# Attention's prologue: four projection banks, masks behind the first two x, and the third half's projections between units of the first pass

## What is computed

```python
x_proj = x @ Wqkv + bqkv
q = x_proj[:, :, :C].reshape(B, n_head, T, hd)
k = x_proj[:, :, C:2 * C].reshape(B, n_head, T, hd)
v = x_proj[:, :, 2 * C:].reshape(B, n_head, T, hd)
att = jnp.einsum('bhtd,bhsd->bhts', q, k) * (1.0 / jnp.sqrt(jnp.float32(hd)))
att = jnp.where(causal, att, jnp.float32(-jnp.inf))
att = jax.nn.softmax(att, axis=-1)
y = att @ v
```

## Time and profile before

| | us |
|---|---|
| median of three runs | 4287.35 (4271.38 to 4290.11) |
| the profiled execution | 4282.62 |
| its span in the trace | 4280.6 |

### The profile page before, as it was taken

How to read it: one execution, slowest core, us unless ns; L and a number is a source line. 1 busy time by engine, 2 the same in 40 slices (tenths; PEclk the granted TensorE clock), 3 DMA queues, 4 the chain that set the end, 5 groups by cost and what they waited for, 6 DMA issues and landing times. The chain is left out here.

```text
span 4280.6 us, 82568 instructions
## 1 busy us (share of the span) xinstructions
PE 3904.8 (91%) x28814; PEld 2547.7 (60%) x28814; DVE 2990.3 (70%) x7504; ACT 2260.4 (53%) x4454; POOL 1340.7 (31%) x1724
## 2 busy tenths in 40 slices
PE   5997899998399999999999999999999996999997
PEld 4886666665255555555555555555555553666664
DVE  6996456565287787777777777777777772466565
ACT  0110455555145666666665666666666663555554
POOL 2332132232524343233432434334342310132322
PEclk9998899999689999999999999999999998999999
DMA  1333111111666686766767767677776631021111
GB/s 56 98 101 96 35 60 47 53 55 35 133 87 109 100 119 103 116 96 98 114 98 102 117 102 107 101 115 105 105 120 104 100 48 56 30 65 55 59 35 45
DMA packets 701476, 361.45 MB, mean 84 GB/s; under 512 B 305072, under 2 KB 668080, under 8 KB 701104
## 3 DMA queue, kind: packets, MB, share of 16 engines
q1 hardware_dynamic: 701104, 356.65, 46.8%
HBM read 204.49 MB, written 150.99 MB: 83 GB/s over the span
## 5 line engine op out<-in xcount | busy, mean ns | idle before, releaser
L1600 DVE TENSOR_REDUCE att_maxima<-att_s 128x1 f32<-128x512 f32 (+3 forms) x3072 | 1523.6, 550 | 421.3 <-PE att_s L1776 224.4
L1698 ACT ACTIVATE att_probs<-att_s 128x512 f32<-128x512 f32 (+1 forms) x2560 | 1330.7, 557 | 896.5 <-PE att_s L1776 507.7
L1830 PE MATMUL att_s<-att_qs,att_ks 49*128 49x512 f32 (+3 forms) x3072 | 1002.2, 402 | 71.9 <-DVE att_maxima L1600 40.9
L1806 PE MATMUL att_s<-att_ks,att_qs 48*128 48x512 f32 (+3 forms) x3072 | 997.7, 409 | 2.1 <-DVE att_maxima L1600 1.6
L1830 PEld LDWEIGHTS att_s<-att_qs,att_ks 49*128 49x128 f32 x3072 | 474.4, 186 | 631.4 <-ACT att_probs L1698 409.2
L1858 PE MATMUL att_o_ps<-att_probs,att_vs 128*32 128x512 f32 (+3 forms) x6144 | 637.4, 500 | 6.0 <-issue 5.5
L1776 PE MATMUL att_s<-att_mask,att_places 64*128 64x64 bf16 (+1 forms) x5632 | 591.8, 209 | 1.8 <-issue 1.8
L1806 PEld LDWEIGHTS att_s<-att_ks,att_qs 48*128 48x128 f32 x3072 | 506.0, 188 | 17.0 <-DVE att_maxima L1600 8.5
L1070 PE MATMUL ffn_h2p<-ffn_h,ffn_w 128*128 128x512 f32 x768 | 382.1, 622 | 2.3 <-ACT ffn_h L947 0.5
L1776 PEld LDWEIGHTS att_s<-att_mask,att_places 64*128 64x128 bf16 x5632 | 284.0, 96 | 113.3 <-issue 43.1
L1517 POOL TENSOR_TENSOR att_x_res<-att_x_res,att_bp_row 128x512 f32<-128x512 f32 x64 | 81.5, 1284 | 772.9 <-DMA att_x_res<-x 770.0
(11 more groups left out here) (227 smaller groups left out, 5782.7 us busy)
## 6 DMA issues: line engine op xcount, KB each, us to landing
att_staged<-qk_scratch SPq DMA_DIRECT2D x768, 128.0 KB, 7.2
qk_scratch<-att_parts SPq DMA_DIRECT2D x128, 512.0 KB, 2.9
ffn_x<-x SPq DMA_DIRECT2D x64, 512.0 KB, 4.9
ssm_x<-in_L_attn_a_x_dram SPq DMA_DIRECT2D x32, 512.0 KB, 3.9
x<-ssm_y SPq DMA_DIRECT2D x32, 512.0 KB, 2.9
x<-ffn_y SPq DMA_DIRECT2D x32, 512.0 KB, 2.9
att_x<-x SPq DMA_DIRECT2D x32, 512.0 KB, 13.4
v_scratch<-att_v_tok SPq DMA_DIRECT2D x32, 512.0 KB, 3.4
```

The lines of the kernel that those rows point to most:

```text
L1600: last = v.tensor_reduce(maxima_of[p][:, g, blk, 1 if t0 else 0:2 if t0 else 1], s1_ps[(2 * unit + 1 - g) % 3][:, col:col + w], AX.X, ALU.max)
L1698: a(probs[u % 2][2 * g + p][:, 0:n], bank[:, 0:n], ACT.Exp).then_inc(exp_done, 1)
L1806: last = mm(bank[:, col:col + w], rows_of(qs[buf], g, KROWS, p, BT * blk, BT * (blk + 1)), rows_of(ks[buf], g, KROWS, p, t0, t1), start=k ...
L1830: last = mm(bank[:, col:col + w], rows_of(ks[buf], g, SHIFT + 1, p, BT * j, BT * (j + 1)), rows_of(qs[buf], g, SHIFT + 1, p, t0, t1), star ...
```

## The change

- `x_bank(index)`: the first 22 projection steps go round four banks, `x_ps` and the three banks of the second pass. Two new semaphores, `low_free` and `v_free`, count banks freed in the prologue by VectorE and by ScalarE; later waits on `x_free` count from the prologue's end.
- GpSimd clears the staging buffers, normalises halves 0 and 1, and then clears and draws masks (`make_masks`); its wait for the weight loads comes behind that. Half 2 is normalised ahead of quad 1's layout.
- VectorE takes the statistics of half 0 ahead of the weights.
- TensorE projects two halves, waits for the masks, and puts one step of half 2 behind every third unit of quad 0's first pass; VectorE's `low` follows in the same places.
- SP waits for the cleared buffers (const_ready) behind the first part's store, and stores half 2's parts around the two moves of maxima.

```diff
+        prologue_ps = [x_ps, *s2_ps]
...
+        def x_bank(index):
+            return prologue_ps[index % len(prologue_ps)] if index < X_PROLOGUE else x_ps
...
                 load_x(1, 1)
-                sp.wait_ge(const_ready, 4)
                 for hb in range(3):
                     for j in range(4):
                         store_part(hb, hb % 2, j)
...
                                 load_x(hb + 2, hb)
+                            if hb == 0:
+                                sp.wait_ge(const_ready, 4)
                         if j % 2 and hb < 2:
                             load_stack(2 * hb, hb, hb, 0, j // 2)
+                        if hb == 2 and j in (0, 3):
+                            move_max(0, 0, j // 3)
...
-                    if hb == 1:
-                        for p in range(2):
-                            move_max(0, 0, p)
...
-                pool.wait_ge(loaded, 16 * len(loads))
+                pool.wait_ge(mask_zero, 2)
                 normalise(0, 0)
                 normalise(1, 1)
+                make_masks()
+                pool.wait_ge(loaded, 16 * len(loads))
                 for hb in range(2):
                     for side in range(2):
                         lay_out(2 * hb, side, False)
+                    for e in range(2):
+                        v_bias(hb, e, 8 * hb + 6 + e)
                     if hb == 0:
-                        for e in range(2):
-                            v_bias(hb, e, 6 + e)
+                        normalise(2, 0)
                         for side in range(2):
                             lay_out(1, side, False)
-                    else:
-                        for e in range(2):
-                            v_bias(hb, e, 14 + e)
-                    if hb == 0:
-                        normalise(2, 0)
...
                 dve.wait_ge(zero_max, 1)
+                prepare(0, 0, 0)
                 dve.wait_ge(loaded, 16 * len(loads))
...
-                prepare(0, 0, 0)
                 prepare(1, 1, 0)
-                for hb in range(3):
+                for hb in range(2):
                     for j in range(6):
                         low(hb, j, 8 * hb + j)
                     if hb == 0:
                         prepare(2, 0, 1)
                 for unit in range(UNITS1):
                     maxima(0, unit)
+                    if unit % 3 == 2:
+                        low(2, unit // 3, 16 + unit // 3)
...
-                    if not isinstance(index, int) or index > 0:
-                        pe.wait_ge(x_free, index)
+                    bank, old = x_bank(index), index - len(prologue_ps)
+                    if index > X_PROLOGUE:
+                        pe.wait_ge(x_free, index - X_PROLOGUE)
+                    elif 0 <= old < X_PROLOGUE - len(prologue_ps) and old % 8 < 6:
+                        pe.wait_ge(low_free, 6 * (old // 8) + old % 8 + 1)
+                    elif 0 <= old < X_PROLOGUE - len(prologue_ps):
+                        pe.wait_ge(v_free, 2 * (old // 8) + old % 8 - 5)
+                    if index < X_PROLOGUE and j == KT:
+                        pe.wait_ge(low_free, 6 * hb + KT)
...
-                pe.wait_ge(weights_ready, 2)
+                for hb in range(2):
+                    for j in range(8):
+                        if hb == 0 and j == KT:
+                            pe.wait_ge(weights_ready, 2)
+                        project(hb, hb % 2, j, 8 * hb + j)
                 pe.wait_ge(mask_ready, 20)
-                for hb in range(3):
-                    for j in range(8 if hb < 2 else 6):
-                        project(hb, hb % 2, j, 8 * hb + j)
                 for unit in range(UNITS1):
                     for g in (1, 0):
                         pass_one(0, 0, unit, g)
+                    if unit % 3 == 2:
+                        project(2, 0, unit // 3, 16 + unit // 3)
```

More of the change, by code:

```diff
@@ L1453, in _ @@
                 g.memset(staged[1][:, :, :], -1.0).then_inc(const_ready, 1)
[L1454 to L1481, removed]
                 def normalise(hb, s):
@@ L1508, in lay_out, with make_masks @@
                     last.then_inc(laid_out[side], 1)
+                def make_masks():
+                    for m in (places[:, :, :], mask[:, :, :, :]):
+                        g.memset(m, 0.0).then_inc(mask_zero, 1)
+                    for s in range(2):
+                        g.memset(vs[s][:, :, HD:32], 0.0).then_inc(mask_zero, 1)
+                    pool.wait_ge(mask_zero, 6)
+                    for s in range(2):
+                        g.memset(vs[s][:, :, HD:HD + 1], 1.0).then_inc(const_ready, 1)
+                    pool.wait_ge(const_ready, 4)
+                    drawn = Chain(pool, mask_ready)
+                    for group in range(2):
+                        rows, row = slice(GROUP * group, GROUP * (group + 1)), slice(GROUP * group, GROUP * group + 1)
+                        for half in range(2):
+                            m = places[rows, half, :]
+                            drawn(g.affine_select(out=m, in_=m, pattern=[[-1, P]], compare_op=ALU.not_equal, fill=1.0,
+                                                  base=GROUP * half, channel_multiplier=1))
+                            m = places[rows, 2 + half, :]
+                            drawn(g.affine_select(out=m, in_=m, pattern=[[1, P]], compare_op=ALU.not_equal, fill=1.0,
+                                                  base=1 - GROUP * (1 + half), channel_multiplier=1))
+                        m = mask[rows, 0, :, :]
+                        drawn(g.affine_select(out=m, in_=m, pattern=[[0, 2], [1, GROUP]], compare_op=ALU.is_ge, fill=-1e30,
+                                              base=0, channel_multiplier=-1))
+                        m = mask[rows, 1, :, :]
+                        drawn(g.affine_select(out=m, in_=m, pattern=[[0, 2], [-1, GROUP]], compare_op=ALU.is_ge, fill=-1e30,
+                                              base=GROUP - 1, channel_multiplier=-1))
+                        drawn(g.memset(places[row, :, :], 0.0))
+                        drawn(g.memset(mask[row, :, :, :], -1e30))
+                        drawn(g.memset(places[row, 0, GROUP:P], 1.0))
+                        drawn(g.memset(places[row, 3, 0:GROUP], 1.0))
@@ L1583, in low @@
                     dve.wait_ge(hi_ready, 6 * hb + j + 1)
+                    bank, freed = x_bank(index), low_free if index < X_PROLOGUE else x_free
                     if j < KT:
-                        v.tensor_tensor(xnT[1][:, j, :], x_ps[:, :], xnT[0][:, j, :], ALU.subtract).then_inc(x_free, 1)
+                        v.tensor_tensor(xnT[1][:, j, :], bank[:, :], xnT[0][:, j, :], ALU.subtract).then_inc(freed, 1)
                     else:
                         j -= KT
-                        v.scalar_tensor_tensor(out=parts[:, j, 1, :], in0=x_ps[:, :], scalar=b_qk[:, j:j + 1],
+                        v.scalar_tensor_tensor(out=parts[:, j, 1, :], in0=bank[:, :], scalar=b_qk[:, j:j + 1],
                                                in1=parts[:, j, 0, :], op0=ALU.add, op1=ALU.subtract).then_inc(parts_ready, 1)
                         dve.wait_ge(parts_ready, 4 * hb + j + 1)
-                        v.memset(carrier[:, :], 0.0).then_inc(x_free, 1)
+                        v.memset(carrier[:, :], 0.0).then_inc(freed, 1)
                 def maxima(quad, unit):
@@ L1700, in project @@
                 def project(hb, j, index):
+                    bank = x_bank(index)
                     act.wait_ge(x_full, index + 1)
                     if j < KT:
-                        a(xnT[0][:, j, :], x_ps[:, :], ACT.Copy).then_inc(hi_ready, 1)
+                        a(xnT[0][:, j, :], bank[:, :], ACT.Copy).then_inc(hi_ready, 1)
                     elif j < 6:
@@ L1707, in project @@
                             act.wait_ge(side_stored[j // 2], 32 * hb)
-                        a(parts[:, j, 0, :], x_ps[:, :], ACT.Identity, bias=b_qk[:, j:j + 1]).then_inc(hi_ready, 1)
+                        a(parts[:, j, 0, :], bank[:, :], ACT.Identity, bias=b_qk[:, j:j + 1]).then_inc(hi_ready, 1)
                     else:
@@ L1867, in project @@
                         pe.wait_ge(xn_ready, hb + 1)
-                    if not isinstance(index, int) or index > 0:
-                        pe.wait_ge(x_free, index)
+                    bank, old = x_bank(index), index - len(prologue_ps)
[7 more added lines that the diff above has]
+                        pe.wait_ge(low_free, 6 * hb + KT)
                     if j < KT:
                         for t in range(TT):
-                            last = pe.transpose(x_ps[:, t * P:(t + 1) * P], xt[s][:, t, j * P:(j + 1) * P], identf[:, :])
+                            last = pe.transpose(bank[:, t * P:(t + 1) * P], xt[s][:, t, j * P:(j + 1) * P], identf[:, :])
                     elif j < 6:
@@ L1875, in project @@
                         for n, (f, (i, k)) in enumerate((f, part) for f in range(KT) for part in PARTS_R):
```

(4 more changed lines are left out.)

23 lines of the change are left out of this document (14 added, 9 removed).

## The result

The changed kernel took 4252.35 us (median of 5 runs, 4244.95 to 4265.45) beside 4283.18 us for the kernel before (5 runs, 4271.38 to 4290.11): ratio 0.992, 95% interval [0.9893, 0.9947]. Forecast were 4274 us and 4258 to 4290. It is faster by more than the 0.5% that I took as the measurable step, to which I gave 0.13.

The account below looks back on a forecast made before the run. The prediction took SP's queue of landings and layout casts to bound attention's prologue. Head 8.1 plus banks 1.3 less tail 1.0 gave 8.4 us, off a profiled 4282.6 us: forecast 4274, range 4258 to 4290.

Parts of the forecast that it names:

- Nothing behind step 1 is touched: Code after step 1 of attention's second pass: claimed unaffected, so the whole gain is the prologue's 8.4 us.
- if spans after step 1 differ by more than 3 us: Sign set against the forecast: later spans, after the second pass's step 1, changing by over 3 us.
- Only the second set of row maxima ... still waits for VectorE: SP's queue before the second pass: from 1142.72 to 1190.92 no step waits for TensorE or VectorE, only issues from 1191.59.
- The head: Start of attention: masks behind two normalisations, statistics ahead of weights; SP's second store at 1105.6 against 1113.67, 8.1 us gained.
- the collision: Head of attention: VectorE's weight preparation held by GpSimd's four tensor_scalar until 1091.0, done at 1094.2 instead of 1089.3.
- rival A: SP's ring and port kinder: no weight hold-up, no sitting store behind the v load; 16.7 us, about 4266; chance 0.17.
- The banks: Prologue projections: four banks end TensorE's wait for its own low part; worth 1.3 us on SP, the rest hidden.
- The tail: SP's queue from second v load to step 1: 19.8 us against 18.8 before, so 1.0 us given back.
- the interleave: Third half between first-pass units: takes 19.1 us and a 5.8 us wait off TensorE's line; SP binds instead.
- B: Rival, slower: second moves on SP's queue stand behind three 512 KB stores, up to 15.8 us; 4290; chance 0.13.
- C: Rival: SP's transfers pack tighter too, TensorE and VectorE bind at 1183 instead of 1209.8; 26.8 us, 4256; chance 0.07.
- D: Rival: no effect, the head's gain lost in a later wait, such as for const_ready or masks; 4282; chance 0.10.

Follow-up runs that it names:

- a_waits64: The changed kernel with 64 idle waits on TensorE ahead of its steady sequence; 4257.48 us, ratio 0.9956.
- banks_only: The kernel before with the four banks alone, head, SP's order and third half as before; the banks alone gave 8.1 us of prologue.
- a_in_a_row: The changed kernel with its third half in a row ahead of the first pass and both sets of moves ahead of the third half's stores; mean 4252.2 us.
- head_only: The kernel before with masks behind two normalisations, statistics ahead of the weights, and the waits for cleared buffers and masks moved; prologue 144.7 us.
- a_moves_early: The changed kernel with both sets of moves of row maxima ahead of the second v store and v load; 4235.32 us, ratio 0.9903; again 4237.76, 0.9917.
- a_copy: The changed kernel once more, no edit; 4251.2 us, ratio 0.9942.
- b_late: The kernel before with five clears of a staging buffer ahead of attention's first load; 4275.91 us, ratio 1.0015.

## Why the prediction was wrong

**The account.** Forecast and median lie 21.9 us apart, and four parts make it up. (a) I took the sum off one execution of 4282.6 us. The runs of the kernel before that stood beside the experiments, 114 of them, have a mean of 4273.0 us and a standard deviation of 12.2: 9.6 us of base. (b) The prologue gave 10.0 us on average (154.46 less 144.43) instead of 8.4: 1.6 us. (c) 36 runs of the change, its copies and a_waits64 have a mean of 4256.6, which is 16.4 us under before's (standard error 2.1), so 6.4 us (2.5) are left for shared code. (d) The five runs' median is 4.2 us under that mean. The first comparison's 30.8 us was thus half chance: before had drawn high, the change low.

**The step that failed** is "Nothing behind step 1 is touched", with the range built on it, "the spread of the runs". True of the code, it was not true of the time. Code that nothing touches differs by 27 us between copies, and I had one trace and three runs, from 4271 to 4290, as if these were its spread. With the base at 4273.0 the same sum gives 4264.6, and a range of the same width about it, 4248 to 4280, holds the median and the mean; (a) alone thus decides, and it needs no mechanism of the change. (c) taken away would bring the median to 4258.8, just inside. (d) does not decide: the mean of 4256.6 lies outside the range too. The line "if spans after step 1 differ by more than 3 us" as a sign against the forecast was of no use, for a copy fails it too.

**What of (c) is shown.** The mean granted clock of the 36 runs is 0.9584, of before's 114 runs 0.9570. Across before's own runs a higher clock of 0.001 goes with 2.2 us less; so 3 of the 6.4 us go with the clock. That it is the change that raises it isn't shown: the three kernels of before with idle waits lie 4.0 us (standard error 2) under before's mean with a prologue no shorter (155.3). A remainder of some 4 us thus may also come with edits that have nothing to do with the change, while before's copies show none (24 runs, 4275.6). Its cause stays open.

**Point by point.**
The sum follows the wrong path for the kernel before. "Only the second set of row maxima ... still waits for VectorE", I wrote, and then counted along SP's queue all the same. The first set waited too (its first move goes out at 1191.59, 0.03 us after its transpose), and what step 1 of before hung on was the end of the first pass, not the second v load. That the count gave 8.4 us was luck, as the terms show.

The head was nearly right in its sum (8.1 us, measured 9.8), and wrong in its parts. The statistics were there earlier (GpSimd's first step at 1083.32, where I had 1084.5), but the batch of tensor_scalar took 6.42 us, not 4.83 as in the earlier trace rows. I had put the collision on VectorE. It fell on GpSimd: VectorE's weight work went through from 1085.71 to 1088.99 while GpSimd's batch stretched by 1.60 us, against 4.82 for the next one. The aggregation behind it stood 1.02 us until the batch ended, but that is no collision: `prepare` waits for xn_ready before it writes half 1's moments, in the kernel before as well, where the same aggregation stood 7.00 us and started at 1099.42 behind the batch of the earlier trace rows. By the Trainium skill (SBUF — State Buffer, "Who interferes with whom") the port pair is locked for one instruction at a time; the trace agrees with that and not with my whole batch from the earlier trace rows. So the projection began at 1094.81 and not at 1097.6, and SP's second store at 1101.51 and not at 1105.6, as rival A has it. Yet the stack loads followed only 4.6 us behind that store (2.8 before), and the second v load was at 1181.36, forecast 1181.5: what TensorE won, SP's transfers kept.

The banks are a term that was mis-sized: 1.3 us forecast, 7.9 measured on top of the head. Some 3 of them show at the second v load (130.5 us behind the FFN in banks_only, 134.0 in the mean of before, whose traces run from 132.1 to 137.3; 121.1 in a_in_a_row, 124.2 in head_only). The other 5 are the moves, which no longer wait for VectorE. I had read that wait in the earlier trace rows, and then priced the new tail against 18.8 us as if that were all issue and landing.

The tail was the matching error on the other side. "1.0 us is given back" was 7.6 us, 2.2 for the interleave and 5.4 for the stores ahead of the moves. Its rows came out as I had put them: the store behind the v load sat 4.28 us (I had 4.4), the moves took 5.57 and 6.58 (5.3 each), the tail 20.0 in all (19.8). So 19.8 was right and the 18.8 it was held against was not: with the moves first it would have been 15.8. An error of 6.6 us in the banks and one of 6.6 us in the tail cancelled, which was luck.

The interleave bought nothing in the change itself: in a_in_a_row, too, the maxima are ready before SP comes to them, by 4.4 us for the first set and 1.5 for the second. Only a_moves_early makes use of it.

**The rivals.** A came half true, with no gain of its own. B's place was right and its price far too high: three stores in 1.88 us, and 1.71 us from the start of the last move to step 1, in the change as in before. C's time came out (4256), but not its mechanism; that one needs the moves to go ahead of the v store and v load, and a_moves_early shows it, with step 1 at 1180.2 where C had TensorE and VectorE bind at 1183. D is out: head_only alone brought 9.8 us to step 1.

## What to carry to other kernels

Before a range is given, ask how far two runs of the same program lie apart, and from how many runs one knows it; take the base from their mean and not from the profiled execution. If a sum has a term for what a queue no longer waits for and another for what it is given to do, an experiment with each part alone is worth more than a total that fits. And a small transfer that the next stage waits for goes ahead of every bulk transfer on its queue as soon as its data are ready: here both sets of moves, 16 issues of 1 KB, were worth 20 us. Before a term is priced along one queue, look at what released the last issue on it: if it was another engine, that engine's path is the one to sum.

## What was not expected of the hardware

TensorE stops for 1 to 3.5 us at fixed places of its program, with no wait in it, in some executions and not in others, and behind many such stops its granted clock stands at 0.50 for as long as 20.5 us. Half-clock stretches come without a stop too. a_copy, where TensorE was busy 4.23 of the 5 us ahead:

```profile
1940.00:1945.00 5.00, 4.23 (x50) 2.44 (x52) 4.01 (x8) 3.31 (x7) 0.00 (x0) 0.99 0.62 213
1945.00:1950.00 5.00, 4.86 (x42) 2.87 (x34) 3.25 (x8) 2.07 (x4) 0.00 (x0) 0.50 1.25 135
```

The runs of one kernel have a standard deviation of 12 us in 4273, which is 0.3%, and a trace has up to 111.9 us at half clock behind step 1. A half-clock microsecond goes with 0.50 us of time, as it would if TensorE were the bound throughout.

A store that SP issues right behind a v load of 512 KB sits: 4.41 us in the earlier trace rows, 4.28 in the change. It is not the store's own cost. In banks_only, where a move of 1 KB stands there, that move sits as long, and the 15 behind it take 0.63 to 0.66 us each:

```profile
1186.52 4.09 SPq L1369 DMA_DIRECT2D att_qs<-att_row_max_T  x1
```

In the kernel before, the first move went out 0.67 us behind the v load and sat 3.90 us; in head_only 2.37 us behind it, and sat 2.11; in b_late 4.40 us behind it, and did not sit. So the next issue, whatever it is, was through no earlier than some 4.5 us behind the v load's start (a move issued there within 2.4 us ended 4.48 to 4.63 us behind it, in nine traces), and the 4.4 us that I had counted against the store in the tail would have fallen on the first move in its place.
